# Attention scores laid out with keys in partitions, and a softmax that VectorE turns in 32x32 squares

## What is computed

```python
# x: (4, 512, 1024), ctx: (4, 64, 1024); 32 query heads, 8 key/value heads, head size 128
x = x + tanh(g_xattn) * attention(layernorm(x), ctx, ctx, Wq, Wk, Wv, Wd)
x = x + tanh(g_ffn) * ffn(layernorm(x), ...)          # int8-like quantised SwiGLU, inner size 512

queries, keys = rope(q @ Wq.T), rope(k @ Wk.T)        # keys, values: 64 rows, repeated for 4 query heads each
scores = einsum('bhqd,bhkd->bhqk', queries, keys) * 128 ** -0.5
scores = where(causal, scores, min)                   # key <= query; queries beyond 63 see all 64 keys
attn = softmax(scores)
out = (attn @ values) @ Wd.T
```

## Time and profile before

| | |
|---|---|
| three runs, us | 1484.33, 1485.55, 1486.3; median 1485.55 |
| profiled execution, us | 1490.73, of which the span is 1488.9 |
| mean granted TensorE clock | 0.993 |
| busy, share of the span | TensorE 96%, VectorE 68%, GpSimd 41%, ScalarE 38% |
| the chain that ended last | TensorE 79%, VectorE 12%, ScalarE 3%, the rest 2% each or less |
| instructions of the probabilities' way through memory | 60 stores of 256 KB, 240 loads of 64 KB |

### The profile page before, as it was taken

The page is one execution under the profiler, slowest core; times in us unless marked ns, Lnnn a source line. Parts: engine busy times, 40 slices in busy tenths (PEclk is TensorE's granted clock), DMA queues, the critical chain, the costliest instruction groups (busy, mean ns, idle before and its releaser), DMA issues.

```text
span 1488.9 us, 19163 instructions
## 1 busy us (share of the span) xinstructions
PE 1431.8 (96%) x7248; PEld 1169.9 (79%) x7248; DVE 1005.5 (68%) x1563; ACT 563.2 (38%) x864; POOL 614.7 (41%) x429
## 2 busy tenths in 40 slices
PE   7999999999999999999999999999999999997887
PEld 7878888888888888887878888888888888874443
DVE  5866575757576766667475757566666666677997
ACT  4424141414242323244542423232322323147995
POOL 3435242434343343440343433434433434233784
PEclk9999999999999999999999999999999999998999
DMA  8834343433425243437265242433333334464565
GB/s 296 251 95 107 72 114 72 106 88 82 112 64 119 68 106 80 108 78 238 74 177 137 70 107 61 95 76 94 83 89 86 94 72 108 93 206 148 120 128 99
DMA packets 327131, 166.52 MB, mean 112 GB/s; under 512 B 275200, under 2 KB 290048, under 8 KB 326656
## 3 DMA queue, kind: packets, MB, share of 16 engines
q1 hardware_dynamic: 324448, 154.29, 39.0%
q0 software_dynamic: 2592, 11.01, 4.5%
HBM read 132.74 MB, written 35.65 MB: 113 GB/s over the span
## 4 chain that ended last, share of the span: by engine, by line
PE 79%; DVE 12%; ACT 3%; DMA 2%; issue 2%; POOL 2%; SPq 1%; ACTq 0%; POOLq 0%; DVEq 0%
PE psum L561 16%; PE psum L563 16%; PE psum L562 16%; PE psum L615 8%; PE psum L650 7%; PE psum L652 7%; PE psum L651 7%; DVE psum L1625 2%; DVE vw_lo L1354 1%; DVE res L1672 1%; DMA acc<-in_x 1%; DMA wv_raw<-in_wv_t 1%; DVE xg L1635 1%; POOL rot L1239 1%; DVE pt_lo L1354 1%
## 5 line engine op out<-in xcount | busy, mean ns | idle before, releaser
L561 PE MATMUL psum<-xt_hi,wq_hi 128*128 128x512 f32 x1024 | 402.1, 393 | 2.6 <-DVE xt_lo L1354 2.6
L562 PE MATMUL psum<-xt_lo,wq_hi 128*128 128x512 f32 x1024 | 399.7, 390 | 0.0
L563 PE MATMUL psum<-xt_hi,wq_lo 128*128 128x512 f32 x1024 | 399.7, 390 | 0.0
L1211 POOL TENSOR_TENSOR wq_lo<-wq_raw,wq_hi 128x512 fp32r<-128x512 f32 x128 | 170.0, 1340 | 490.7 <-ACT wq_hi L918 490.7
L1515 DVE TENSOR_TENSOR acc<-psum,acc 128x512 f32<-128x512 f32 x224 | 151.3, 681 | 140.3 <-PE psum L652 140.3
L1239 POOL TENSOR_TENSOR rot<-rot 128x1024 f32<-128x1024 f32 x64 | 153.5, 2399 | 207.8 <-DVE rot L1458 207.0
L561 PEld LDWEIGHTS psum<-xt_hi,wq_hi 128*128 128x128 f32 x1024 | 193.1, 189 | 42.2 <-DVE xt_lo L1354 2.8
L563 PEld LDWEIGHTS psum<-xt_hi,wq_lo 128*128 128x128 f32 x1024 | 192.9, 188 | 40.8
L964 ACT ACTIVATE vw_hi<-psum 64x512 fp32r<-64x512 f32 x256 | 151.4, 591 | 194.0 <-PE psum L563 190.3
L562 PEld LDWEIGHTS psum<-xt_lo,wq_hi 128*128 128x128 f32 x1024 | 192.9, 188 | 39.5
L1354 DVE TENSOR_TENSOR vw_lo<-psum,vw_hi 64x512 fp32r<-64x512 f32 x256 | 175.4, 686 | 52.9 <-ACT vw_hi L964 46.8
(11 more groups left out here) (151 smaller groups left out, 1915.8 us busy)
## 6 DMA issues: line engine op xcount, KB each, us to landing
wq_raw<-in_wq_t SPq DMA_DIRECT2D x128, 256.0 KB, 4.4
wd_raw<-in_wd_t SPq DMA_DIRECT2D x128, 256.0 KB, 3.6
p_scratch<-prob SPq DMA_DIRECT2D x60, 256.0 KB, 2.0
pt_raw<-p_scratch SPq DMA_DIRECT2D x240, 64.0 KB, 2.5
acc<-in_x SPq DMA_DIRECT2D x16, 512.0 KB, 5.5
out_x<-acc SPq DMA_DIRECT2D x16, 512.0 KB, 3.9
xa<-out_x SPq DMA_DIRECT2D x16, 512.0 KB, 3.6
out_x<-res POOLq DMA_DIRECT2D x15, 512.0 KB, 5.5
```

The costliest lines, as they stand in the source:

```text
L561: pe.matmul(dst, a_hi, b_hi, start=start, stop=False)
L562: pe.matmul(dst, a_hi, b_lo, start=False, stop=False)
L563: return pe.matmul(dst, a_lo, b_hi, start=False, stop=stop)
L1211: pool.tensor_tensor(dst, full, hi.bitcast(F32), ALU.subtract).then_inc(done, 1)
```

## The change

Scores are made with `kblk` as the stationary operand and `rot` as the moving one: two matmuls of 512 columns in place of eight of 128. The score bank then has 2 x 64 keys in partitions and 512 tokens in columns. VectorE turns all 32x32 squares of it (from PSUM to `prob`), so that each square has tokens in partitions and 32 keys in its columns. Maximum and sum over 32 keys come from a reduction per square; the other 32 keys of the same head lie in the neighbouring quadrant of 32 partitions, so four copies (`other_half`) bring its values across and one more instruction combines them. After the multiplication a second turn gives the probabilities with keys in partitions, straight into `pt_raw`. `move_probs`, `turn_probs` and the scratch tensor are gone. The score waits for the first turn of the unit before (`st_done`), not for its subtraction.

Beside it: the rotation tables lose their third part, and `add_turned` becomes a subtraction and an addition of 512 columns each. At the start ScalarE makes the statistics of the last two tiles (`late_statistics`). In the first group of a half values part 2 goes from the third slot to the fourth. In the third slot `lower_probs` goes ahead of `softmax_b`. In the feed-forward loop the second normalisation is prepared in two parts, with four of the sums of squares at steps 4 to 7, and GpSimd scales `v_sd`.

```diff
             def score(unit):
                 b = unit % 2
+                if unit:
+                    pe.wait_ge(st_done, unit)
...
-                if unit:
-                    pe.wait_ge(sub_done, unit)
...
-                for t in range(BT):
-                    for j in range(2):
-                        ins = pe.matmul(scores[:, t * P:(t + 1) * P], rot[:, 0, j, t * P:(t + 1) * P],
-                                        kblk[:, j, 2 * b:2 * b + 2, :].rearrange("p a k -> p (a k)"), start=(j == 0), stop=(j == 1))
+                for j in range(2):
+                    keys = kblk[:, j, 2 * b:2 * b + 2, :].rearrange("p a k -> p (a k)")
+                    ins = pe.matmul(scores, keys, rot[:, 0, j, :], start=(j == 0), stop=(j == 1))
                 ins.then_inc(s_done, 1)
...
                 if kind == 3 and not filled:
-                    for part in range(1, 4):
-                        queries(unit, part)
+                    queries(unit, 1)
+                    values(gg, 2)
+                    queries(unit, 2)
+                    queries(unit, 3)
...
-                turn_probs(unit - 2)
                 values(gg - 1, 6)
...
-                turn_probs(unit - 1)
...
+            def late_statistics():
+                last, junk = slice(HTILES - 2, HTILES), bank(O_BANK, 2)
+                act.wait_ge(xt_lo_done, 2)
+                for t in (HTILES - 2, HTILES - 1):
+                    act.wait_ge(x_in[t], 16)
...
+                    act.activation(junk, acc[:, t, :], ACT.Copy, accum_out=mv[:, t, 0:1]).then_inc(late_done, 1)
...
+                    act.activation(junk, acc[:, t, :], ACT.Square, scale=-1.0, bias=mv[:, t, 0:1], accum_out=mv[:, t, 1:2]).then_inc(late_done, 1)
...
                 if s == 2:
-                    down_columns()
-                if s < 4:
-                    deviations(1, 2 * s)
-                    deviations(1, 2 * s + 1)
-                if s == 4:
-                    root(TILES + 2, slice(HTILES, TILES))
+                    root(TILES + 2, slice(HTILES, HTILES + BT))
+                if BT <= s < HTILES:
+                    deviations(1, s)
+                if s == HTILES:
+                    root(TILES + 3, slice(HTILES + BT, TILES))
...
-                pool.tensor_tensor(rot[:, 0, :, :], rot[:, 0, :, :], rot[:, 1, :, :], ALU.add).then_inc(rope_done, 1)
+                pool.tensor_tensor(rot[:, 0, 0, :], rot[:, 0, 0, :], rot[:, 1, 1, :], ALU.subtract)
+                pool.tensor_tensor(rot[:, 0, 1, :], rot[:, 0, 1, :], rot[:, 1, 0, :], ALU.add).then_inc(rope_done, 1)
...
+            pool.tensor_scalar(v_sd[:, :], v_sd[:, :], gates[:, 1:2], 1.0, ALU.mult, ALU.mult).then_inc(vd_done, 1)
...
+            def other_half(part, done):
+
+                for a in range(4):
+                    there_rows, rows = slice(32 * (a ^ 1), 32 * (a ^ 1) + 32), slice(32 * a, 32 * a + 32)
+                    ins = dve.tensor_copy(other[there_rows, part // 2, :], tops[rows, part, :])
+                ins.then_inc(done, 1)
...
             def softmax_a(unit):
 
                 dve.wait_ge(s_done, unit + 1)
-                view = scores[:, 0:P].rearrange("p (h k) -> p h k", h=2)
-                dve.tensor_tensor(view, view, cst[:, C_MASK:C_MASK + KEYS].unsqueeze(1).broadcast_to([P, 2, KEYS]),
-                                  ALU.add).then_inc(mask_done, 1)
+                dve.tensor_tensor(scores[:, 0:KEYS], scores[:, 0:KEYS], cst[:, C_MASK:C_MASK + KEYS], ALU.add).then_inc(mask_done, 1)
                 dve.wait_ge(mask_done, unit + 1)
-                view = scores.rearrange("p (s k) -> p s k", k=KEYS)
-                dve.tensor_reduce(red[:, 0, :], view, AX_X, ALU.max).then_inc(max_done, 1)
+                dve.transpose(prob[:, :, :], blocks(scores)).then_inc(st_done, 1)
+                dve.wait_ge(st_done, unit + 1)
+                dve.tensor_reduce(tops[:, 0, :], prob[:, :, :], AX_X, ALU.max).then_inc(max_done, 1)
+
+            def softmax_less(unit):
+
                 dve.wait_ge(max_done, unit + 1)
...
-                dve.tensor_tensor(prob[:, :, :], view, red[:, 0, :].unsqueeze(2).broadcast_to([P, 2 * BT, KEYS]),
+                other_half(0, top_in)
+                dve.wait_ge(top_in, unit + 1)
+                dve.tensor_tensor(tops[:, 1, :], tops[:, 0, :], other[:, 0, :], ALU.max).then_inc(top_done, 1)
+                dve.wait_ge(top_done, unit + 1)
+                dve.tensor_tensor(prob[:, :, :], prob[:, :, :], tops[:, 1, :].unsqueeze(2).broadcast_to([P, TB, 32]),
                                   ALU.subtract).then_inc(sub_done, 1)
...
+                dve.tensor_reduce(tops[:, 2, :], prob[:, :, :], AX_X, ALU.add).then_inc(sum_step, 1)
+                dve.wait_ge(sum_step, 5 * unit + 1)
+                other_half(2, sum_step)
+                dve.wait_ge(sum_step, 5 * unit + 2)
+                dve.tensor_tensor(tops[:, 3, :], tops[:, 2, :], other[:, 1, :], ALU.add).then_inc(sum_step, 1)
...
+                dve.transpose(pt_raw[:, :, :], prob[:, :, :]).then_inc(pt_done, 1)
```

More of the change, by code:

```diff
@@ L47 @@
 BT = SEQ // P
+TB = SEQ // 32
 UPG = 2 * HB
@@ L488, in _ @@
                             next_wd(VPG * gg + i)
-                    if u >= 1 and moved(unit - 1):
-                        move_probs(unit - 1)
                     if u % UPG == 3:
```

210 lines of the change are left out of this document (95 added, 115 removed).

## The result

| | before | changed |
|---|---|---|
| median, us (runs) | 1485.92 (4) | 1569.17 (4; 1567.55 to 1575.73) |
| profiled execution, us (its span) | 1490.73 (1488.9) | 1567.55 (1565.5) |
| mean granted TensorE clock | 0.993 | 0.979 |

The account below looks back on a forecast made before the run. TensorE was taken as nearly full, with VectorE's fixed-order chain at most 0.18 us from delaying it. 37.8 + 7 + 11 - 3 - 2.4 - 2.1 - 2 - 1.5 = +44.8 us on a 1485.55 median gave 1530, range 1505 to 1550.

Parts of the forecast that it names:

- Elsewhere the same added time falls into pauses: Hand-overs outside (a), (b) and (c): VectorE's added time costs nothing; 14 x 0.3 us or so if one cover were gone.
- (a): Hand-over from a group's fourth unit to the next's first: TensorE waits 2.7 us more, 14 times, +37.8 us.
- (b): Second unit of a group: output part 7 waits 0.5 us for the sixth addition, 14 times, +7 us.
- (c): Last unit of each half: 3.0 + 4.1 - 1.6 = 5.5 us longer, twice, +11 us, bounds 6 and 14.
- Part 2: TensorE's score blocks: 2 matmuls of 512 columns for 8 of 128 gain 0.05 us each, -3 us in all.
- Rival 3: Score blocks: short records are paced by weight loads, so a block takes 0.91 us and the total is 1476; chance 0.07.
- Part 3, memory: Probabilities' stores and loads vanish: nothing in the first half, late hand-overs of the second half go, -2.4 us.
- Part 4: Moved work: values part 2 in the first group -2.1 us, the start -2, the feed-forward part -1.5.
- The feed-forward edits: Feed-forward part, squares moved to steps 4 to 7: some 5 us gained early, 4 given back, -1.5 us.
- 1 (overlapping copies): VectorE's copies between quadrants overlap at 0.09 us each, 15 us less than forecast, 1515 us; chance 0.15.
- rival 4: The added VectorE work hides in its 26 idle us a group, only gains remain, 1475 us; chance 0.03.
- 2: GpSimd and pt_lo collide on the chain at (a) or (b), 15 us more than forecast, 1545 us; chance 0.12.

Follow-up runs that it names:

- e1: The changed kernel with VectorE's second turn of the queries moved ahead of the softmax sums in a group's fourth slot: 1534.37 us.
- e3: The changed kernel with each exchange between quadrants as one copy in place instead of four across, so maximum and sum cover half the keys: 1525.15 us.
- e2: The changed kernel with ten unread 512-column matmuls on TensorE ahead of the score of every filled first slot: 1563.27 us.
- e5: e1 with addition 5 ahead of pt_lo in second slots, and second turn and ScalarE's values part 5 weight split earlier in each half's first group: 1521.76 us.
- e6: The changed kernel with the start's statistics and order, and the feed-forward edits, taken back: 1564.16 us.
- e11: The changed kernel with each of the eight copies between quadrants done twice: 1659.13 us.
- e9: e8 with more reordering of VectorE's queue and two of ScalarE's copies of values earlier: 1486.14 us, ratio 1.0001 to the kernel before.
- e8: e5 with the feed-forward part and the start of before, and the last unit of each half in another order: 1501.96 us.

## Why the prediction was wrong, point by point

Three steps of the sum failed. It took a wait of TensorE at its length, with nothing for the clock behind it (measured +9.2). It put the added VectorE time at nothing outside the filled groups ("Elsewhere the same added time falls into pauses") and counted a gain at the start (forecast -4.1 for the first groups, measured +9.6). And it sized the ends at 11 (measured 17.9).

1. **What bounds the kernel** (right). VectorE's fixed order with 0.18 us of slack at the hand-over was the place; e1 removes the whole wait with one moved call.
2. **Prices on VectorE** (right, near). Forecast 1.62 ahead of the first turn, 0.97 behind, 2.59 together. Measured 1.66 and 1.04, 2.71 along the chain. The copies stand at 0.72 for four, 0.76 with the gap (0.73 taken), the first turn out of PSUM at 0.75 (0.74), the combining one at 0.21 (0.22). The reciprocal and the scaling, at 0.27 and 0.24 on 16 columns in PSUM, are 0.06 slower together than on 8 columns, where I had 0.02. By the Trainium skill ("VectorE: DVE Perf Modes", section on two Vector instructions with no wait between them) copies that start in another quadrant are held one behind the other; the trace agrees with 0.17 each, none starting before the one ahead has ended, and e3 shows their price on the path.
3. **(a) The hand-over** (mechanism right, count off). 2.69 a time for 2.7, but 12 times, not 14: the first hand-over of a half comes out of a group without filling and belongs to the start. That made the sum 5.5 too high here, and by luck hid as much of what it lacked elsewhere.
4. **The missing term.** The sum took a wait at its length. Six of twelve waits cost 1.4 to 1.7 us more, since TensorE's clock had fallen, 9.2 in all; e2 shows that this goes with the idling, and e3 that a single 1.49 of it is too short. My range had no term for it, though the earlier trace rows held the sign: behind the wait of 5.16 the block of eight took 3.57, where its followers take 1.90 in the changed kernel's rows above.
5. **(b) The addition** (right): 0.62 for 0.5, fourteen times.
6. **(c) The last units** (11 forecast, 17.9 measured). The step that failed is "3.0 + 4.1 - 1.6 = 5.5". The last but one pt_lo starts 13.5 us behind its slot's score instead of 10.2, and takes 1.77 where I had it at 0.68, since GpSimd's split of the last weights runs beside it. So the wait that I counted as gone (0.6 to 0.8) became 5.86, and the following output runs at the lower clock (0.50 from 709 to 713 us). The additions stand behind the longer softmax too: 3.64 and 1.41 of waiting.
7. **Part 2, the score block** (right to 1.7 us): -1.3 for -3. Rival 3 is out: 1.72 a block.
8. **Part 3, memory** (right). The late hand-overs of half two are gone: all are 17.41.
9. **Part 4, the start** (sign wrong): +5.6 for -4.1. I priced which waits would go and not what the new softmax does in slots without filling, where the scores follow each other by 12.7 to 18.7 us instead of 20 to 22. There the score waits 2.28 and 1.30, and in half two 1.15, 1.38 and 1.05. Of the two waits of the earlier trace rows the 2.60 went and 2.70 for `far` came; the 2.09 went, but 1.81 for wd_lo stands in the fourth slot, to which values part 2 was moved, and that slot's step grew from 15.87 to 19.12. e5 takes 4.3 of it back, e6 shows that the statistics made at most 0.9 of it. "Elsewhere the same added time falls into pauses" failed here, and in e1 and e11 at the second and fourth slot.
10. **The feed-forward edits** (sign wrong): +2.6 for -1.5. The early gain is 2.2 instead of 5; the part given back, 4.8, was near my 4.
11. **Rivals.** 1 (overlapping copies) and 3 (records paced by loads) are refuted by the rows; 4 by the result, though e9, at 1486 where rival 4 had 1475, shows that in another order the added VectorE work costs next to nothing. 2 is half true: pt_lo does collide with GpSimd, 1.76 in the hand-over and 0.94 on the mean of all 64 (0.97 before the change), but in the hand-over behind the second turn, where nobody waits for it; on a path it was at the ends.

In numbers: 9.2 (clock) + 9.7 (start) + 6.9 (ends) + 4.0 (first group of half two) + 4.1 (feed-forward) + 1.6 (b) + 1.7 (score) - 5.5 (count in a) is 31.7 of the 31.8 between 44.8 and the 76.6 of the two spans. The medians stand 83 apart, since the profiled execution of before lay 5 above its median and the changed kernel's 1.6 below.

## What to carry over

Work added to an engine that is idle a third of the time costs what its order makes of it: find the hand-over with the least slack, and move the call that others wait for ahead of the added work; here one moved call gave back 35 of 83 us, and some twenty, with the start and the feed-forward part of before, all of it. Price a new pause of TensorE at more than its length once the pauses of the profile show slow records behind them. And price it in every form of the loop, the unfilled first pass and the last one too, since the shortest pass has the least cover.

## What the runs showed of the hardware

- **The clock and short pauses.** In groups where TensorE otherwise waits no more than 0.3 us at a time, pauses of 1.49 us left the granted clock at 1.00 twelve times of twelve (e3); pauses of 2.56 were followed by records at the 1.2 GHz level six times of twelve, in turn in the changed kernel and out of turn in e6; pauses of 4.1 twelve of twelve, in a kernel with other waits of up to 1.3 (e11). The 2.28 ahead of the second score of the changed kernel brought the clock down as well (0.66 over the 4 us from 102.5), the 1.30 ahead of the third didn't. What picks the six of twelve stays open. Several short pauses close together did it too: 1.50, 1.52 and 1.41 within 7 us in the feed-forward part, and the block behind them took 3.60 instead of 1.90. Filled with unread matmuls until 0.34 was left of it, the pause of 2.56 cost no clock (e2).
- **Small instructions of VectorE beside GpSimd.** In e8 two instructions on 128x8 in SBUF took 1.20 where they take 0.17 in e9; GpSimd ran a 128x512 subtraction at that moment:

```profile
666.90 1.20 DVE L1397 TENSOR_SCALAR newton<-newton 128x8 f32<-128x8 f32 x1
668.14 1.20 DVE L1399 TENSOR_TENSOR rstd<-newton 128x8 f32<-128x8 f32 x1
```
```profile
666.81 1.27 POOL L1188 TENSOR_TENSOR wq_lo<-wq_raw,wq_hi 128x512 fp32r<-128x512 f32 x1 [0.23 <-ACT wq_hi L884]
668.03 1.29 POOL L1188 TENSOR_TENSOR wd_lo<-wd_raw,wd_hi 128x512 fp32r<-128x512 f32 x1
```
```profile
677.02 0.17 DVE L1397 TENSOR_SCALAR newton<-newton 128x8 f32<-128x8 f32 x1
```

  The trace agrees with the Trainium skill ("SBUF — State Buffer", section on two separate sides), by which a VectorE instruction with two SBUF inputs, or in a mode that uses both ports, shares a lock with GpSimd, and the one that comes second waits until the other has ended. Both end 0.02 behind GpSimd's, at 668.10 (GpSimd 668.08) and 669.34 (669.32), whatever their own size. The first has one input; which mode it ran in the trace doesn't show. pt_lo, with two SBUF inputs, shows the same on a large one: at 1.76 and 1.77 it ends 0.55 behind GpSimd's.
